# Attention beside a ternary layer: loads and tables of chunk 0 reordered, ternary tiles placed by attention's progress

## The reference, cut to what matters

```python
xn = layernorm(x)                                  # x: 2048 x 256
q, k, v = xn @ Wq, xn @ Wk, xn @ Wv                # 8 heads, 2 key/value heads, 32 wide
q, k = rope(q, cos, sin), rope(k, cos, sin)
std = softmax(causal(q @ k.T * scale)) @ v
geo = softmax(causal((q[:3] . dirs) * (k[:3] . dirs))) @ v
att = (std + head_scales * (geo - std)) @ Wo
z = xn @ ternary(W_syn).T + b_syn                  # 2048 x 1024
hidden = where(z >= the 102nd largest z of the row, relu(z), 0)
ffn = layernorm(xn + hidden @ ternary(W_out).T + b_out, gamma, beta)
out = x + att + ffn
```

## Time and profile before

| | |
|---|---|
| median of 3 runs | 775.68 us (774.01 to 776.37) |
| profiled execution | 776.62 us, span 774.9 us |
| mean granted TensorE clock | 0.927 |
| busy: PE, PE weight loads, DVE, ACT, POOL | 694.9, 327.5, 498.3, 449.4, 226.8 us |
| DMA | 35.46 MB in 26931 packets |
| geometric / standard attention, chunk 2 | from about 284 / 397 us |
| geometric / standard attention, chunk 3 | from about 493 / 628 us to 755 us |
| first and last `y` of the ternary layer | 488.4 and 734.6 us |

### The profile page before, as it was taken

The page is one execution under the profiler, slowest core; times in us unless marked ns, Lnnn a source line. Parts: engine busy times, 40 slices in busy tenths (PEclk is TensorE's granted clock), DMA queues, the critical chain, the costliest instruction groups (busy, mean ns, idle before and its releaser), DMA issues.

```text
span 774.9 us, 12300 instructions
## 1 busy us (share of the span) xinstructions
PE 694.9 (90%) x4424; PEld 327.5 (42%) x4424; DVE 498.3 (64%) x974; ACT 449.4 (58%) x733; POOL 226.8 (29%) x304
## 2 busy tenths in 40 slices
PE   0857988799999999969999999999999989998993
PEld 0533444334244443423343444554544445654532
DVE  3782786856675876558567696567665567767602
ACT  1655345344334442468444445799989989996550
POOL 3431314531111212111010120452343453247232
PEclk9965899679899998989999999999989999999996
DMA  9494038240000000160000000000000000000000
GB/s 238 150 280 134 1 128 209 77 102 1 1 7 1 1 1 1 32 158 1 0 3 3 1 1 3 22 22 28 28 22 22 28 22 28 16 22 8 1 1 27
DMA packets 26931, 35.46 MB, mean 46 GB/s; under 512 B 7090, under 2 KB 21298, under 8 KB 26483
## 3 DMA queue, kind: packets, MB, share of 16 engines
q1 hardware_dynamic: 21874, 33.80, 15.0%
q10 hardware_dynamic: 4992, 0.84, 0.6%
HBM read 20.08 MB, written 13.89 MB: 44 GB/s over the span
## 4 chain that ended last, share of the span: by engine, by line
PE 62%; DVE 10%; issue 5%; ACT 3%; POOL 3%; DMA 3%; SPq 1%; DVEq 0%; ACTq 0%; POOLq 0%
PE acc L1420 14%; PE acc L1413 14%; PE side L1312 10%; PE scores L1395 7%; DVE piece_max L1126 4%; PE scores L1399 3%; DMA q_stack<-q_parked 3%; PE side L1366 2%; PE side L1357 2%; PE side L1374 2%; PE side L1367 2%; ACT probs L889 2%; PE side L1349 2%; PE side L1350 1%; POOL probs L746 1%
## 5 line engine op out<-in xcount | busy, mean ns | idle before, releaser
L889 ACT ACTIVATE probs<-scores 128x1024 f32<-128x1024 f32 (+3 forms) x320 | 271.0, 893 | 230.9 <-PE acc L1420 208.3
L1126 DVE TENSOR_REDUCE piece_max<-side 128x1 f32<-128x512 f32 x189 | 125.3, 685 | 78.9 <-PE side L1312 77.5
L1413 PE MATMUL acc<-probs,v_nat 128*32 128x512 f32 (+3 forms) x1280 | 158.1, 568 | 8.7 <-POOL probs L746 8.5
L1420 PE MATMUL acc<-probs,ones_all 128*32 128x512 f32 (+3 forms) x1280 | 156.8, 564 | 0.0
L1312 PE MATMUL side<-k_stack,q_stack 96*128 96x512 f32 (+3 forms) x309 | 122.5, 450 | 17.0 <-DMA q_stack<-q_parked 9.2
L746 POOL TENSOR_SCALAR_AFFINE_SELECT probs<-probs 128x256 f32<-128x256 f32 x128 | 60.8, 484 | 243.8 <-ACT probs L889 242.5
L1312 PEld LDWEIGHTS side<-k_stack,q_stack 96*128 96x128 f32 x309 | 55.5, 199 | 106.2 <-issue 52.4
L1395 PE MATMUL scores<-q_stack,k_stack 98*128 98x512 f32 (+3 forms) x320 | 92.5, 393 | 1.5 <-ACT probs L889 1.3
L1129 DVE CUSTOM_DVE_ANT_0 side<-side,tail_mask 128x256 f32<-128x256 f32 (+3 forms) x120 | 57.7, 488 | 33.3 <-PE side L1312 32.8
L1413 PEld LDWEIGHTS acc<-probs,v_nat 128*32 128x32 f32 x1280 | 37.2, 114 | 86.9 <-issue 64.8
L1152 DVE RECIPROCAL d_raw<-d_raw 128x512 f32<-128x512 f32 x16 | 53.6, 3347 | 23.2 <-ACT o_raw L902 23.2
(11 more groups left out here) (165 smaller groups left out, 911.1 us busy)
## 6 DMA issues: line engine op xcount, KB each, us to landing
q_stack<-q_parked SPq DMA_DIRECT2D x12, 512.0 KB, 8.0
q_parked<-turned SPq DMA_DIRECT2D x8, 512.0 KB, 3.0
trig_parked<-probs SPq DMA_DIRECT2D x3, 768.0 KB, 5.2
trig<-trig_parked SPq DMA_DIRECT2D x3, 768.0 KB, 4.3
res<-in_L_attn_x_dram SPq DMA_DIRECT2D x4, 512.0 KB, 8.9
x_parked<-xn SPq DMA_DIRECT2D x4, 512.0 KB, 3.2
xT_parked<-xnT SPq DMA_DIRECT2D x4, 512.0 KB, 5.2
xb<-x_parked SPq DMA_DIRECT2D x16, 128.0 KB, 2.0
```

What stands on the lines that cost most here:

```text
L889: nc.scalar.activation(probs[:, slot % 2, pair, :, off:], scores[:, pair, :, off:], ACT.Exp, scale=ATT_SCALE if kind == 0 else 1.0).then_i ...
L1126: free(nc.vector.tensor_reduce(piece_max[:, h, p:p + 1], pt, AX.X, ALU.max), ("S",) + a)
L1413: nc.tensor.matmul(acc[D * h:D * h + D, 0, off:], v_nat[:, j, g], probs[:, slot_no[a] % 2, h // 2, h % 2, off:], start=(j == 0), stop=(j = ...
L1420: last = nc.tensor.matmul(acc[D * h:D * h + D, 1, off:], ones[:, 0:D], probs[:, slot_no[a] % 2, h // 2, h % 2, off:], start=(j == 0), stop ...
```

## The change

Loads. On ACT's queue Wq, Wk, Wv come first, then the tables of chunk 0 only; on SP's queue x of chunk 0 and the small table come first, then SP waits for the weights before it issues x of chunk 1, W_syn and the rest. Tables of chunk c > 0 are loaded by SP (`ang_in`) when the third transpose of chunk c - 1 is done, into a buffer of their own; `spread` goes into the third slot of `turned`, once the k parts of the chunk before are parked; `t_put` writes straight to `trig`, once the projections of the chunk before are read. `trig_parked` and its six transfers are gone.

Order. Statistics of chunk c > 1 wait for `m` of chunk c - 2, `geo_lo` and `scan` of chunk c > 0 for `m` of chunk c - 1. `w_cut` is parted into `w_mean` (the threshold) and `w_cut` (the passes), with a semaphore `ternary_ready` in place of the bank's; `w_mean` of W_out waits for `m` of chunk 0. W_out, `xz_in` and `xb_in` are issued behind `stack_lo` of chunk 0. `xs_hi` of tile t waits for the attention step at which the share 0.02 + 0.85 t / 16 of attention is done. The search and `hide` get rank 2 on DVE, `wsum` and `wT` rank 1.5 instead of 0 on TensorE. One memset of DVE at the start (L1004) is gone.

```diff
+LEAD = 0.02
+REACH = 0.85
+Z_RANK = 11
+H_RANK = 10
+F_RANK = 2
+W_UNIT = 1.5
...
+        if c:
+            add("ang", "sp", 2, ("ang_in", c), 1100, [("unit", "tT", c - 1, 2)])
         for s in range(3):
-            rank = 0 if c == 0 else 0.5
+            rank = 0 if c == 0 else 2 * c - 0.5
+            slots_free = [("khi_park", c - 1), ("klo_park", c - 1)] if c else []
...
-            add("trig", "act", rank, ("t_put", c, s), 600, [("unit", "tT", c, s)] + [("t_park", c - 1)] * (c > 1), empties=("tT", c, s))
+            add("trig", "act", rank, ("t_put", c, s), 600, [("unit", "tT", c, s)] + [("rope", c - 1, k) for k in "ABK"] * (c > 0),
+                empties=("tT", c, s))
...
-    add("w_sort", "dve", 0, ("w_sort",), 2000, [("w",)])
+    add("w_sort", "dve", 0.2, ("w_sort",), 2000, [("w",)])
...
-            add("stat", "dve", STAT_RANK if c else 0, ("stat", t), 650, [("x", c)])
+            add("stat", "dve", STAT_RANK if c else 0, ("stat", t), 650, [("x", c)] + [("m", c - 2)] * (c > 1))
...
+        due = [("m", c - 1)] if c else []
...
-        add("geo", "dve", rank, ("geo_lo", c), 1220, [("geo_hi", c)] + old)
-        add("geo", "dve", rank, ("scan", c), 2800, [("geo_in", c)] + old)
+        add("geo", "dve", rank, ("geo_lo", c), 1220, [("geo_hi", c)] + old + due)
+        add("geo", "dve", rank, ("scan", c), 2800, [("geo_in", c)] + old + due)
...
-            add("w", "sp", 0, ("w_next",), 500, [("w_cut", 0)])
+            add("w", "sp", 0, ("w_next",), 500, [("w_cut", 0), ("stack_lo", 0)])
...
-        unit("w", 0, ("wsum", m), 60, [("w_abs", m)])
-        add("w", "dve", W_RANK, ("w_cut", m), 4400, [("unit", "wsum", m)] + [("w_put", 0, 3)] * m, empties=("wsum", m))
+        unit("w", W_UNIT, ("wsum", m), 60, [("w_abs", m)])
+        add("w", "dve", 2, ("w_mean", m), 560, [("unit", "wsum", m)] + [("m", 0)] * m, empties=("wsum", m))
+        add("w", "dve", W_RANK, ("w_cut", m), 3900, [("w_mean", m)] + [("w_put", 0, 3)] * m)
...
+    share = [1 - max(0, j - TPC * c) / TPC for c, g, kind, j in slots]
+    turn = []
+    for t in range(NT):
+        due = LEAD + REACH * t / NT
+        turn.append(next(slot for n, slot in enumerate(slots) if sum(share[:n + 1]) >= due * sum(share)))
...
-        add("z", "act", Z_ACT, ("xs_hi", t), 400, [("xz_in", t), ("w_cut", 0)] + [("unit", "z", t - 1, 1)] * (t > 0))
+        add("z", "act", Z_ACT, ("xs_hi", t), 400, [("sum",) + turn[t], ("xz_in", t), ("w_cut", 0)] + [("unit", "z", t - 1, 1)] * (t > 0))
...
-        add("pick", "dve", 5, ("pick", t, 0), 1750, [("sign", t, 2)] + [("unit", "hT", t - 1, 1)] * (t > 0))
+        add("pick", "dve", F_RANK, ("pick", t, 0), 1750, [("sign", t, 2)] + [("unit", "hT", t - 1, 1)] * (t > 0))
...
-        add("pick", "dve", 4, ("hide", t), 2750, [("unit", "found", t)], empties=("found", t))
+        add("pick", "dve", F_RANK, ("hide", t), 2750, [("unit", "found", t)], empties=("found", t))
...
             sp.dma_start(res[:, 0:TPC], x_rows[0]).then_inc(x_in[0], 16)
+            sp.dma_start(small[:], small_table.broadcast_to([P, H * 3 + RANKS])).then_inc(dir_in, 16)
+            sp.wait_ge(w_in, N_W_IN)
             sp.dma_start(res[:, TPC:2 * TPC], x_rows[1]).then_inc(x_in[1], 16)
-            sp.dma_start(small[:], small_table.broadcast_to([P, H * 3 + RANKS])).then_inc(dir_in, 16)
...
+                if k == "ang_in":
+
+                    c = key[1]
+                    sp.wait_ge(side_full, unit_no[("tT", c - 1, 2)] + 1)
...
-            act.dma_start(angles[:, :, 0:HALF], cos_table[:, 0:HALF].rearrange("(t p) d -> p t d", p=P)).then_inc(ang_in, 16)
-            act.dma_start(angles[:, :, HALF:], sin_table.rearrange("(t p) d -> p t d", p=P)).then_inc(ang_in, 16)
             for w, at in ((Wq, 0), (Wk, H * D), (Wv, QK)):
                 act.dma_start(w_given[:, :, at:at + w.shape[1]], w.rearrange("(k p) n -> p k n", p=P)).then_inc(w_in, 16)
+            act.dma_start(angles[:, :, 0:HALF], cos_table[0:CHUNK, 0:HALF].rearrange("(t p) d -> p t d", p=P)).then_inc(ang_in, 16)
+            act.dma_start(angles[:, :, HALF:], sin_table[0:CHUNK].rearrange("(t p) d -> p t d", p=P)).then_inc(ang_in, 16)
...
-            free(nc.scalar.copy(trig[:, s] if c == 0 else trig_next[:, s], pt), ("tT",) + a)
+            free(nc.scalar.copy(trig[:, s], pt), ("tT",) + a)
```

116 lines of the change are left out of this document (54 added, 62 removed).

## The result

The changed kernel takes 766.32 us (764.82 to 772.45 in four runs) against 776.02 us: a ratio of 0.989, 95% interval 0.9852 to 0.9929. It is faster, as forecast, and inside the range, but by 9.7 us where the forecast had 20. The profiled execution took 764.82 us, span 762.7; it is the fastest of the four, while before's (776.62) is slower than all of its timed runs, so the two profiles lie 11.8 us apart and not 9.7.

A forecast was written before the change was run, and what follows sets the result against it. The prediction took TensorE's work, its idle time and a low clock to bound the kernel. Terms -13 - 3 + 3 - 7 + 5 - 5 = -20 gave 756 us, with a range from 738 to 773.

The forecast's parts named there:

- (A): Early loads: weights first and a quarter of the tables bring the first projection near 16 us; -13 us.
- The Trainium skill's rival: Early loads: weights and tables land late at a higher packet price, first rope about 25 us; 762 us, chance 0.05.
- (B): Wait for chunk 0's stack: dropping the tables' HBM round trip and later loads lighten DMA; -3 us.
- (C): W_out made ternary after chunk 0's maxima: its work leaves idle DVE time for a busy stretch; +3 us.
- (D): Held statistics and geo chain: idle time and clock in 135 to 200 us improve, -7; a second gap costs +5.
- The +5: Cost of a second stretch without S matmuls, TensorE waiting for the stack; between 0 and 8 us.
- the second gap: Expected new stretch without S matmuls, some 25 us near 200 us, where ternary tiles could find banks.
- (E): Gated ternary tiles, search at rank 2: some 4 to 6 of 16 tiles done before the last chunk; -5 us.
- rival 1: Ternary tiles still find no bank, so spreading fails and only the early gain stays; 768 us, chance 0.20.
- Rival 3: Search waits on in-order DVE stall the row maxima and stop TensorE among S tiles; 782 us, chance 0.10.
- (F): Tail: 10.46 us of TensorE waiting for reciprocal and mix, then the output projection, stays; 0 us.

The follow-up runs named there:

- e4: Changed kernel with 40 extra throwaway identity products, 20 ahead of everything and the rest behind early transposes; 766.56 us, ratio 0.9897.
- e13: Kernel before with only W_out held back behind chunk 0's maxima and stack, tables first and parked; 782.86 us, ratio 1.0099.
- e1: Changed kernel with the old load order: tables of all chunks ahead of the weights, no wait on SP; 780.28 us, ratio 1.0057.
- e10: e9 plus W_out held back behind chunk 0's maxima and stack, tables still parked; 771.03 us, ratio 0.992.
- e9: Kernel before with only the load order changed, weights first, tables still parked; 788.06 us, ratio 1.0169.
- e6: Changed kernel with W_out loaded and made ternary as early as before; 776.19 us, ratio 1.0014.
- e14: Changed kernel with tables loaded first and W_out early again, tables still built per chunk; 788.23 us, ratio 1.0201.
- e5: Changed kernel without the rules holding later chunks' statistics and geo chain behind earlier maxima; 767.45 us, ratio 0.9895.
- e3: Changed kernel with TensorE ranks of z and h at 2.5 and 2.4 instead of 11 and 10; 785.93 us, ratio 1.0158.
- e11: Changed kernel with ternary tiles no longer gated by attention and the search's ranks back at 5 and 4; 770.38 us, ratio 0.993.
- e8: Changed kernel with the planner's assumed stack landing at 8000 and 8000 ns instead of 6000 and 4500; 762.75 us, ratio 0.9822.

## Why the prediction was right or wrong, step by step

**(A) Right, with its rows.** Weights landed by 6.88 us (9 was taken, the bounds were 5 and 12), the first projection at 15.65 (16.1), the first rope at 19.44 (19.1). Undone in the changed kernel it costs 14.0 us, where 13 was forecast. The Trainium skill's rival, page "DMA: Bandwidth & Descriptors", section "Bandwidth", would have had the first rope at about 24.8 us; the measured 19.44 is on the side of the trace's price. The 24.8 is an estimate from that page's 10.5 ns per packet, which it gives for transfers issued by GpSimd; no run here bears it out. What the step didn't see: the first 12 projection matmuls are slower than in the kernel before (8.05 us against 3.01 + 3.70, and 5.39 in e4, all at a granted 1.00). And what (A) is worth depends on the rest: 12 to 14 us with tables per chunk, or with parked tables and C, but it costs 11 when put into the kernel before alone.

**(B) -3: the wait went, for another reason.** From the last split to the first S matmul still 50.72 - 30.89 = 19.8 us pass, as before. The last part of the stack was issued at 40.48 and landed 10.1 us later, at 50.6 (before: issued at 56.05, landed 8.1 us later), so the lighter DMA traffic shortened nothing. The 2.92 us of waiting vanished because chunk 1's projection now stands in that time. With W_out late, B (with D and E) is worth 2.6 us with tables first (e13 to e1) and 4.7 with weights first (e10 to after), hardly more than what a new plan alone moves; with W_out early 11.9 (e9 to e6), but -12.2, a loss, out of the kernel before (to e14).

**(C) +3: wrong in sign.** In the changed kernel it measured -10. I called its time before "the wait for the stack and the idle stretch behind it, where DVE is otherwise empty", which was true of the kernel before, and there holding W_out back alone does cost 7 us (e13). I didn't ask what the other parts do to that stretch. (A) takes 12 us of it away: with parked tables it turns what C is worth from +7 (e13) to -17 (e9 to e10). (B) fills it: tables per chunk bring chunk 1's projection and ropes there, from 98 to 58 us even with tables first (e14), and W_out's early work breaks them in two, 37 to 38 us apart. Either is enough, for with (B) C gains with late loads too: 8.0 us (e14 to e1), against 9.9 with early ones (e6 to after). This error doesn't explain the missing 10 us: with -10 in place of +3 the sum would have been -33.

**(D) -7 + 5: the first step that failed.** The rows came, the gain didn't. Chunk 2's projection moved to 182.43, the grant from 135 to 200 rose to 0.95, and the idle time there fell from 6.2 to 2.85 us: some 13 us in that window, more than the 7. But e5, without D, takes 767.45: it has 28.4 us idle before 160 and a clock loss of 32.4 us there against 25.3, and 17.3 against 22.9 behind. What the stretch gave in the clock was given back in others: in windows of 5 us, the clock loss from 135 to 200 us fell from 12.4 in the kernel before to 3.4, and that from 80 to 135 rose from 4.1 to 9.3. A term that is a low clock in one window is no term of the sum. The +5 didn't come either: in the second gap nothing waits for chunk 2's stack, and the wait for chunk 3's is 2.13 us instead of 5.12.

**(E) -5: the second step that failed.** One tile had its y before 493 us, not four, and TensorE is idle for 9.4 us from 493 to the end of attention, as the 9.8 before; the second gap let no more tiles in, because z and h still come last in rank, as rival 1 said. e3 brought the tiles forward by rank, and the time rose by 20 us instead of falling by 5. Rival 3 had that sign, but not its cause: TensorE's idle time rose by only 5 us, most of the rest was clock.

**(F) 0: right.** 10.46 us again.

**The sum, and the term that was missing.** Idle time fell by 20.3 us where the terms added up to 20, yet this is chance. Before 160 us the terms A, B and C gave -13, and the idle time there fell by 20.3. Behind it D and E gave -7, and the idle time there did not fall (22.2 us from 160 to 740 in both kernels). The low clock on the work that moved had no term at all, though I had named it as the second loss and had counted a gain from it in (D): it came to +7.8 us. So the forecast failed in D and E, whose net -7 didn't come, and in the clock, put at nothing. Idle time and clock together give -12.5 us, against -12.2 between the two spans; the medians are 9.7 apart. The result lay nearest to rival 1 (768), for the half of its reason that e11 bears out.

Nor do the terms add up when they are taken back one at a time: A undone costs 14.0 us, C 9.9, and B with D and E 4.7 (e10 to after), 28.6 in all, for a change that gained 9.7. The difference is about the 20 us by which the kernel before is better than the sum of its parts.

**What stays open** is why the kernel before is 7 to 12 us better than each neighbour that differs from it in one part. Late table copies explain part of it for e9. For e13 and e14 the runs show only more idle time before and behind 160 us. Its planner constants may suit its own order, since e8 moved the changed kernel by 3.6 us with two of them, but constants were not tried on e9, e13 or e14, and e14's assume early loads that it doesn't have.

## What to carry to other kernels

When several parts of a change move work, price each at the place where the others have put everything else, and not in the kernel before: in the kernel before, holding W_out's early work back only cost time, and once another part had brought the preparation of chunk 1 from 98 to 58 or 45 us it gained 8 to 10 us. A part can cost time alone and gain it in company: early loads, late W_out and tables per chunk each made the kernel before slower by 7 to 12 us. Count a low granted clock as a cost of the whole kernel, not of the window that shows it, and expect some of the removed idle time back in longer matmuls. Where a planner writes the order, run one or two neighbours of its constants before believing a difference of under 5 us.

## What the runs showed of the hardware

A granted clock won in one stretch was lost in another. Filling 7 us of early idle time with throwaway products (e4: 16.8 us idle before 160, against 23.9) moved the low level of the early stretch from 32 to 44 us (changed kernel) to 26 to 32 us (e4), and left the clock loss of the whole kernel where it was, 47.2 against 48.1 us.

The granted clock doesn't show every slow matmul. The first projection's 12 matmuls took 8.05 us in the changed kernel, where TensorE had executed nothing before 8.00 us, and 5.39 us in e4, where it had been busy from 1.74 us on; the profile gives a grant of 1.00 for both.

The two kernels with the least clock loss have much idle time (e14: 75.2 us idle up to 740, 36.1 us lost; e6: 62.9 and 40.2; the changed kernel 46.1 and 48.1), but idle time alone doesn't decide it (e9: 63.8 and 53.5). Runs of one kernel differ as well: the changed kernel took 764.82 us at a mean grant of 0.924 and 772.45 at 0.911. And the stretch from 40 to 80 us had a mean grant of 0.54 to 0.76 in the kernels shown, even where TensorE was busy for 38.5 of its 40 us: a busy TensorE alone did not hold the 2.4 GHz level.
